# Attention scores computed in four column tiles of 32 keys, spread 5, 5, 3, 3 over a step's quarters, with the denominators moved

## The reference

```python
def _L0_xattn_ref(q, k, v):            # 32 query heads, 8 key heads, D = 32, G = 4
    scores = jnp.einsum('bkgsd,bktd->bkgst', qh, kh) / scale
    weights = jax.nn.softmax(scores, axis=-1)
    out = jnp.einsum('bkgst,bktd->bkgsd', weights, vh)
    ...
x = x + _L0_xattn_ref(_layernorm(x, axis=-1), ctx_512, ctx_512)
x = x + _L0_ffn_ref(_layernorm(x, axis=-1), ...)   # 8 small experts, the one with the largest gate
```

## Time and profile before

| | us |
|---|---|
| median of 3 runs | 1094.2 |
| lowest and highest run | 1093.95, 1095.56 |
| the profiled execution, its own time | 1095.06 |
| its span in the trace | 1093.2 |
| attention steps, by the timeline | 68 to 910 |
| PE, DVE busy | 970.6, 919.3 |
| ACT, POOL busy | 756.3, 774.0 |

### The profile page before, as it was taken

One profiled execution on the slowest core, in us unless ns is written; L12 is line 12 of the kernel. 1 busy time (PEld: TensorE's weight loads), 2 busy tenths in 40 slices (PEclk: granted clock), 3 DMA queues, 4 the chain that ended last, 5 costly groups with the idle time before them and its releaser, 6 DMA issues.

```text
span 1093.2 us, 18664 instructions
## 1 busy us (share of the span) xinstructions
PE 970.6 (89%) x6442; PEld 337.3 (31%) x6442; DVE 919.3 (84%) x1202; ACT 756.3 (69%) x1333; POOL 774.0 (71%) x373
## 2 busy tenths in 40 slices
PE   3269999999999999999999999999999998999994
PEld 2112222222222222222222222222222225776771
DVE  4669999999999899889999999988888874889964
ACT  5348878888788888778878878877767666544430
POOL 2017888888888888888888888888988897111100
PEclk9999999999999999999999999999999999999998
DMA  7744767576767676766666666756455643755322
GB/s 200 203 109 97 163 135 178 136 175 137 172 136 166 133 163 138 165 138 160 143 160 146 164 145 157 156 117 149 105 125 139 154 100 110 248 197 206 139 115 116
DMA packets 324545, 163.88 MB, mean 150 GB/s; under 512 B 187229, under 2 KB 312157, under 8 KB 324453
## 3 DMA queue, kind: packets, MB, share of 16 engines
q1 hardware_dynamic: 324452, 162.70, 60.7%
HBM read 107.84 MB, written 54.53 MB: 149 GB/s over the span
## 4 chain that ended last, share of the span: by engine, by line
PE 45%; DVE 35%; issue 15%; ACT 3%; DMA 1%; POOL 0%; SPq 0%; DVEq 0%; ACTq 0%; POOLq 0%
DVE row_max L809 22%; PE psum L500 10%; PE psum L476 9%; PE psum L488 9%; PE psum L439 5%; PE psum L592 5%; DVE o_t L815 4%; PE psum L573 3%; DVE probs L1004 3%; PE psum L465 2%; DVE prod_mem L868 2%; PE psum L562 1%; DVE stats L837 1%; DMA k_split<-k_parts 1%; DVE k_parts L862 1%
## 5 line engine op out<-in xcount | busy, mean ns | idle before, releaser
L729 ACT ACTIVATE probs<-psum 128x512 f32<-128x512 f32 x1024 | 553.5, 595 | 161.3 <-PE psum L476 156.1
L809 DVE TENSOR_REDUCE row_max<-psum 128x4 f32<-128x2048 f32 x256 | 584.2, 2282 | 39.0 <-PE psum L439 30.5
L280 POOL TENSOR_TENSOR sums<-probs 128x2048 f32<-128x2048 f32 x64 | 290.9, 4546 | 56.6 <-ACT probs L729 56.6
L476 PE MATMUL psum<-q_stack,k_stack 97*128 97x512 f16 x1024 | 317.9, 386 | 12.5 <-ACT probs L729 10.2
L292 POOL TENSOR_TENSOR sums<-probs 128x2048 f32<-128x2048 f32 x64 | 291.6, 4556 | 26.0 <-ACT probs L729 26.0
L488 PE MATMUL psum<-probs,v_in 128*32 128x512 f32 x2048 | 273.6, 606 | 5.1 <-ACT probs L729 2.6
L476 PEld LDWEIGHTS psum<-q_stack,k_stack 97*128 97x128 f16 x1024 | 78.3, 97 | 254.0 <-ACT probs L729 147.0
L439 PE MATMUL psum<-high_mem 32*128 32x512 f16 x1024 | 103.1, 391 | 39.3 <-DVE row_max L809 28.3
L500 PE MATMUL psum<-sums,ones 128*32 128x512 f32 x1024 | 121.6, 592 | 0.0
L821 DVE STREAM_TRANSPOSE den_t<-psum 128x512 f32<-128x512 f32 x64 | 45.9, 717 | 64.7 <-PE psum L500 64.7
L256 POOL TENSOR_TENSOR o_t<-o_t,inv 128x512 f32<-128x512 f32 x64 | 67.2, 1049 | 37.5 <-DVE inv L827 37.5
(11 more groups left out here) (93 smaller groups left out, 703.1 us busy)
## 6 DMA issues: line engine op xcount, KB each, us to landing
q_stack<-q_split SPq DMA_DIRECT2D x192, 128.0 KB, 3.3
xa<-in_x_dram SPq DMA_DIRECT2D x32, 512.0 KB, 3.6
q_split<-prod_mem SPq DMA_DIRECT2D x16, 1024.0 KB, 5.6
o_all<-in_x_dram SPq DMA_DIRECT2D x256, 64.0 KB, 2.3
x_attended<-o_all SPq DMA_DIRECT2D x64, 256.0 KB, 4.4
out_dram<-probs SPq DMA_DIRECT2D x32, 512.0 KB, 2.9
high_mem<-q_split SPq DMA_DIRECT2D x64, 128.0 KB
high_mem<-k_split SPq DMA_DIRECT2D x64, 128.0 KB
```

Of the source, the lines that this page charges most:

```text
L280: pool.tensor_tensor(sums[:, (2 * u - 1) % SUMS], probs[:, (u - 1) % 2, 2], probs[:, (u - 1) % 2, 3], ALU.add).then_inc(back_done, 1)
L476: pe.matmul(st_ps[:, bank_of["score", u, n], :], k_stack[:, u % SLOTS, t * P:(t + 1) * P], q_stack[:, u % SLOTS, g, :], start=True, stop=T ...
L729: act.activation(probs[:, s, t, g, :], st_ps[:, bank_of["score", u, n], :], ACT.Exp, scale=EXP_SCALE).then_inc(exped, 1)
L809: dve.reduce_max(row_max[:, u % 2, t:G * ST:ST], s_ps[:], AX.X).then_inc(reduced, 1)
```

## The change

Four things change, and nothing else.

- A score is computed by four products of 32 keys each, which write the four bands of 32 partitions of the same bank, instead of one product of 128 keys. The last of the four signals.
- The 16 scores of a step are dealt 5, 5, 3, 3 over the quarters (`BEGIN`), and the gather stands after the second score of each quarter (`MIDST`). ACT's exponentials follow, with the waits for a probability block's buffers at the block's first score, the shift before score 12 and the centring pass before score 13 (it was before 14).
- The denominators are cut in two: eight instructions over the first half's sum and eight over the second's. In odd steps all sixteen stand in the fourth quarter, behind the maxima product and before the scores. In even steps the first eight stand at the end of the third quarter and the last eight behind the maxima product of the fourth.
- The bank plan lists the denominators at the end of the third quarter, after score 12, instead of in the fourth between the two pairs.

```diff
+            BEGIN = (0, 5, 10, 13, NSC)
+            MIDST = (2, 7, 12, 15)
...
-                    scores = [("score", u, t * G + g) for g in range(G)] if live(u) else []
+                    scores = [("score", u, n) for n in range(BEGIN[t], BEGIN[t + 1])] if live(u) else []
+                    half = MIDST[t] - BEGIN[t]
...
-                    filled += scores[:2]
-                    if t == ST - 1 and live(u - 1):
-                        filled.append(("den", u - 1, 0))
+                    filled += scores[:half]
                     if t == 2 and live(u + 1):
                         filled.append(("max", u + 1, 0))
-                    filled += scores[2:]
+                    filled += scores[half:]
+                    if t == 2 and live(u - 1):
+                        filled.append(("den", u - 1, 0))
...
-                def score_keys(u, t, pair):
+                def score_keys(u, begin, end):
...
-                        pe.matmul(st_ps[:, bank_of["score", u, n], :], k_stack[:, u % SLOTS, t * P:(t + 1) * P],
-                                  q_stack[:, u % SLOTS, g, :], start=True, stop=True).then_inc(scored, 1)
+                        for row in range(0, P, D):
+                            last = pe.matmul(st_ps[row:row + D, bank_of["score", u, n], :],
+                                             k_stack[:, u % SLOTS, t * P + row:t * P + row + D],
+                                             q_stack[:, u % SLOTS, g, :], start=True, stop=True)
+                        last.then_inc(scored, 1)
...
+                        if t == ST - 1 and live(u - 1) and live(u):
+                            if u % 2 == 1:
+                                first_denominators(u - 1)
+                            last_denominators(u - 1)
                         if u % 2 == 1 and t < PIECES and whole(tile_of(u)):
                             turn_part(tile_of(u), t)
                         if live(u):
-                            score_keys(u, t, 0)
+                            score_keys(u, BEGIN[t], MIDST[t])
...
-                        if t == ST - 1 and live(u - 1) and live(u):
-                            denominators(u - 1)
                         if t == 2 and live(u + 1):
                             turn_max(u + 1)
                         if live(u):
-                            score_keys(u, t, 1)
+                            score_keys(u, MIDST[t], BEGIN[t + 1])
+                        if t == 2 and live(u - 1) and live(u) and u % 2 == 0:
+                            first_denominators(u - 1)
...
-                            for g in range(G):
-                                n = t * G + g
-                                if t == 2 and g == 2 and live(u + 1):
+                            for n in range(BEGIN[t], BEGIN[t + 1]):
+                                keys, g = n // G, n % G
+                                if g == 0:
+                                    wait(act, pv_done, ST * (u - 2) + keys + 1)
+                                    wait(act, front_done if keys < ST // 2 else back_done, u - 1)
+                                if n == MIDST[2] and live(u + 1):
                                     make_shift(u + 1)
-                                if t == ST - 1 and g == G // 2:
+                                if n == BEGIN[ST - 1]:
                                     centring_pass()
```

More of the change, by code:

```diff
@@ L466, in turn_part @@
                     last.then_inc(turned, 1)
-                def score_keys(u, t, pair):
-                    if t == 0 and pair == 0:
+                def score_keys(u, begin, end):
+                    if begin == 0:
                         wait(pe, s_in[u % SLOTS], 96 * (u // SLOTS + 1))
                         wait(pe, shift_in[u % 2], 16 * (u // 2 + 1))
-                    for g in (2 * pair, 2 * pair + 1):
-                        n = t * G + g
+                    for n in range(begin, end):
+                        t, g = n // G, n % G
                         bank_free("score", u, n)
-                        pe.matmul(st_ps[:, bank_of["score", u, n], :], k_stack[:, u % SLOTS, t * P:(t + 1) * P],
-                                  q_stack[:, u % SLOTS, g, :], start=True, stop=True).then_inc(scored, 1)
+                        for row in range(0, P, D):
[3 more added lines that the diff above has]
+                        last.then_inc(scored, 1)
                 def gather(u, t):
@@ L490, in gather, with first_denominators, last_denominators @@
                     last.then_inc(pv_done, 1)
-                def denominators(u):
+                def first_denominators(u):
                     wait(pe, front_done, u + 1)
-                    wait(pe, back_done, u + 1)
                     bank_free("den", u, 0)
                     wait(pe, den_taken, u)
-                    for part in range(2):
-                        for g in range(G):
-                            last = pe.matmul(st_ps[g * D:(g + 1) * D, bank_of["den", u, 0], :], ones[:, 0:D],
-                                             sums[:, (2 * u + part) % SUMS, g, :], start=(part == 0), stop=(part == 1))
+                    for g in range(G):
+                        pe.matmul(st_ps[g * D:(g + 1) * D, bank_of["den", u, 0], :], ones[:, 0:D],
+                                  sums[:, 2 * u % SUMS, g, :], start=True, stop=False)
+                def last_denominators(u):
+                    wait(pe, back_done, u + 1)
+                    for g in range(G):
+                        last = pe.matmul(st_ps[g * D:(g + 1) * D, bank_of["den", u, 0], :], ones[:, 0:D],
+                                         sums[:, (2 * u + 1) % SUMS, g, :], start=False, stop=True)
                     last.then_inc(den_done, 1)
@@ L603, in body @@
                         project(q, 1)
-                        denominators(UNITS - 1)
+                        first_denominators(UNITS - 1)
+                        last_denominators(UNITS - 1)
                     if before:
@@ L719, in _ @@
                             s = u % 2
[L720 to L723, removed]
-                                if t == 2 and g == 2 and live(u + 1):
+                            for n in range(BEGIN[t], BEGIN[t + 1]):
[4 more added lines that the diff above has]
+                                if n == MIDST[2] and live(u + 1):
                                     make_shift(u + 1)
-                                if t == ST - 1 and g == G // 2:
+                                if n == BEGIN[ST - 1]:
                                     centring_pass()
                                 wait(act, scored, NSC * u + n + 1)
-                                act.activation(probs[:, s, t, g, :], st_ps[:, bank_of["score", u, n], :], ACT.Exp,
+                                act.activation(probs[:, s, keys, g, :], st_ps[:, bank_of["score", u, n], :], ACT.Exp,
                                                scale=EXP_SCALE).then_inc(exped, 1)
```

## The result

| | before | after |
|---|---|---|
| median of 6 runs each, us | 1094.88 | 1106.12 |
| lowest and highest run | 1093.95, 1096.68 | 1100.39, 1107.74 |
| the profiled execution, its own time | 1095.06 | 1102.37 |
| its span | 1093.2 | 1100.6 |

The ratio of the means is 1.0089, 95% interval 1.0064 to 1.0114: slower by 0.9% (9.7 us; the medians lie 11.2 us apart), where 4.3 us less were forecast. The time lies inside the range; the sign was wrong.

A forecast was written before the change was run, and what follows sets the result against it. No engine alone bound the kernel: each quarter lasted as long as the longer of PE's and DVE's in-order lists. Terms +34.3, -28.2, -8.9 and -1.5 gave -4.3 us, 1094.2 to 1090; range 1060 to 1112, A's own 1082 to 1092.

The forecast's parts named there:

- SP's order is untouched: SP's issue of the shift row: follows the max, 4.5 before the next step's first score, so no cost.
- Odd steps: Attention steps turning an input tile: 15.10 us against 13.78, +1.32 each, +34.3 over 26.
- The chain over the banks: Odd steps: part 0's bank passes to score 4, then part 1; second quarter 4.15, PE and DVE waiting.
- Even steps: Attention steps between the odd tile steps: 11.54 us against 12.67, -1.13 each, -28.2 over 25.
- Steps without a tile: The ten steps u = 52 to 61: mean 11.87 us against 12.76, -0.89 each, -8.9 together.
- The last two attention steps: End of attention, where PE and ACT run without maxima: -1.5 us, bounds -3 and 0.
- The value taken: PE's scores as four f16 column tiles: 0.215 us per score, lower bound 0.215, upper bound 0.325.
- rival E: Four tiles of a score cost 0.325 on PE, +0.11 each: 1144 us; chance 10%.
- What went and came with the shapes: PE's shape changes: two per quarter at score and gather go (0.2); tile transposes and max transpose to scores gain some.
- the estimated 1107: Total if the skill's 62 ns per matmul held: a score 0.25, 0.03 more than taken; no row could show it.
- D: Rival: slower through part 0's bank chain in odd steps, from odd 15.26; with 0.1 more per hand-over 1105; chance 27%.
- A: Rival, the forecast: odd steps pay some 1.3 (14.8 to 15.2), all others win; 1082 to 1092; chance 30%.

The follow-up runs named there:

- experiment 5: The changed kernel with the shift row sent by ACT on its own DMA queue instead of by SP: 1088.13 us, 0.9943 of the kernel before.
- experiment 1: The changed kernel with the store of the input tiles issued ahead of the unit's loads on SP: 1108.71 us, 1.0133 of the kernel before.
- experiment 3: The changed kernel with another bank plan, no score between the parts of a tile: 1088.22 us, 0.9927 of the kernel before.
- experiment 9: The kernel before with scores as four column tiles and nothing else: 1081.64 us, 0.9880 of the kernel before.
- experiment 11: The kernel before with SP's send of the shift row moved behind the addend's and next input tile's loads: 1250.73 us, 1.1430 of the kernel before.

## Why the prediction was wrong

**The step that failed** is one sentence, costed at 0: "SP's order is untouched; send_shift follows the max, which by the walk stands 4.5 before the next step's first score". The order was untouched indeed, but not the times in it, and what stands ahead of the row was not looked up. The cover was sized about right: from the start of the row's making to the first score there are 5.2 us in an even step and 4.3 in an odd one, where nothing is late. What had to fit into it was not sized at all. At u = 5 the row waits 3.3 us behind the store and the load of v and takes 4.0 to land, 7.3 together.

In the old kernel the same row took 1.6 (129.69 to 131.29) plus 3.4 of the 5.7 that it had. Two things changed. The cover became 0.5 shorter: the making stands 7.86 after an even step's first maxima in both kernels, the next step begins 1.0 earlier, and its first score stands 0.5 later in it. And SP reached the store 1.6 us later in that step, 6.7 after the first maxima instead of 5.1. The row of the odd step before leaves SP 3.7 before the even step begins, where it was 4.6, and the eight addend loads issued behind it run into the even step:

```profile
128.89 0.49 SPq L67 DMA_DIRECT2D high_mem<-q_split  x1
```

This first load of the even step's unit stands 2.67 after the maxima; before, it stood 0.35 after them (122.18). Over all thirteen steps ahead of a wanted row the send came 9.7 to 11.1 after the first maxima, where it had been 8.6 to 9.7.

The size: the profiled spans are 1086.5 in experiment 5 and 1100.6 in the changed kernel, 14.1 us, where the sum had nothing for the row. 12.0 of them lie in the steps behind a store, some 1 of it at u = 5 for the lower clock behind the wait. 1.3 lie in step 0 (15.64 against 14.35), and they are not the row's: its first score stands 0.54 behind the maxima in both. PE's maxima took 0.61 us there until 76.52 in the one and until 71.44 in the other, and 0.40 to 0.45 behind that; the same step took 13.78 in experiment 1 and 13.56 before, and why it varies is open. 0.8 lie elsewhere. In the medians the difference is 18 (1106.1 less 1088.1, with 0.7 between the kernels before beside them), since the profiled execution of the changed kernel was one of its shorter ones.

**The other terms**, measured on experiment 5 against the profile of before, by the first maxima of the steps (span 1086.5 against 1093.2, -6.7):
- Odd steps: +1.08 each against +1.32 (14.86 against 15.10), 23 of them from u = 5 to 49, +24.8. The first quarter was 3.79 instead of 4.0, the fourth 3.75 instead of 3.85, while the second was 4.34 instead of 4.15. The chain over the banks was right in place and cost; experiment 3, which takes it out, brings the step to 13.88.
- Even steps: -1.01 against -1.13, 24 of them, -24.2.
- Steps without a tile: -7.9 together against -8.9.
- The start: steps 0 to 3 were longer by 0.8, 1.64, 0.26 and 0.65, so +3.3, where the prediction charged steps 1 to 3 like all others (+1.5) and step 0 nothing.
- u = 51, the last odd step with a tile: +0.7. The last two attention steps and what follows: -3.1 against -1.5, at its bound. Before step 0: -0.35.
The sum was -4.3 and the kernel without the wait has -6.7. That is near, but the odd steps were charged 0.24 too much each (some 6 us) and the even ones credited 0.12 too much (some 3), and the start and the end were off by about 2 each, in opposite directions.

**The tiles.** The value taken, 0.215 a score, held within 0.01: rival E with 0.325 is out, and experiment 9 shows the tiles alone at 1081.6, faster than the whole change. What went and came with the shapes was right too: score to gather 0.22 instead of 0.32 (491.39 to 491.83 for two), max to score 0.21 (512.29 to 512.50) instead of 0.11. The Trainium skill, TensorEngine Tiling (Array Packing), Restrictions and Gotchas, says that column tiling turns the fast weight load off. The trace can't show whether it did, and shows that it cost nothing where PE had no wait: PEld is busy for 370 us instead of 337, beside the products. The Trainium skill, TensorE: Matmul & The Clock Gate, the section on 56 ns against 53.3, gives some 62 ns for a matmul with hardware decode off. That is not this case: eight products in 0.44 us are 55 ns each, and the estimated 1107 that the rule gave is no explanation of the 1106.

**The rivals.** D's time was 1105 and the run gave 1106, but that is luck and not D, and so is that the range, drawn up to 1112 for D, held the time. It had to have usual odd steps above 15.26, and they are 14.86; the one quarter over its walk is the second, by 0.19. What makes the kernel slower than before is a row that is late by more than 0.3 us in eight odd steps and in step 53. No rival had it. A, with odd steps of 14.8 to 15.2, is the mechanism that ran in 15 of the 23 from u = 5 to 49, and in all 23 once the row was off SP; it was undone by what stood outside it. The prediction's own test (even above 12, odd under 14.8 or over 15.3 make it wrong) passes the usual steps and catches six of the eight irregular ones.

**What stays open.** Why the row takes as long as it does to land. In the odd steps without a store ahead it took 1.6 to 1.8 us in most and up to 3.1; behind a store 2.4 to 4.2, and before the change the same. In experiment 1 it took 1.8 at u = 5, with the store long issued. That points to the store's packets, which go by the same queue (q1 of the trace), but which share is theirs was not measured apart.

## What to carry to other kernels

When an edit shortens a step, list for every DMA that the step waits for what stands ahead of it in the issuing engine's queue, in the step where that queue is fullest, and hold made, issued and wanted against each other; "the order is untouched" is no cost of 0 if the due time moves. A small transfer on which a step's first product waits belongs on a queue with nothing large ahead of it, and the engine that makes its data is a natural place. When the profile names no releaser, ask it for the landing of each transfer that the stalled product reads: the one that lands just before the start is the likely cause. And try the parts of a compound edit alone: here the tiles alone won 1.2%, the order alone (with the row sent by ACT) lost 2.0%, and with another bank plan and the row on another queue the whole wins 3%.

## What was not expected of the hardware

A single long wait of PE can cost more than its own length, and needn't. At u = 5 the first score stood 3.58 behind the maxima, the granted clock had a mean of 0.82 in the quarter, and the quarter took 6.85. At u = 17 the first score stood 3.56 behind them, the clock stayed at 1.00, and the quarter took 5.78: 1.07 less behind an equal wait. At the lower of its two levels, 1.2 GHz, the maxima took 0.61 us instead of 0.40; the gather, part of it at that level, took 1.63 instead of 1.03. In experiment 11 the mean was 0.70 in the quarter shown. What decides whether a wait of this length lowers the clock is not shown here. And 32-column f16 tiles with 97 rows of contraction run at nearly the pace of one whole product, eight pairs of load and product in 0.44 us; from the last of them to the maxima, which have another shape, 0.11 is added (497.81 to 498.14), as before.
